# A fused layer of gated recurrence and mixture of experts: the order of the work ahead of the tile loop is rearranged

## The chip, the cores and the metric

The kernel runs on one core of a Trainium2 chip. It is written in Bass: every engine (TensorE = PE, VectorE = DVE, ScalarE = ACT, GpSimd = POOL, SyncE = SP for transfers) has its own list of instructions, executed in the order in which the code writes them, and the engines meet only at semaphores. The metric is the device time of one execution in microseconds; a smaller one is better. All data is float32.

## The reference

The input is 2 x 1024 tokens of width 256. They are normalised; the normalised rows `xn` feed a gated recurrence in log space and a mixture of 8 experts, two of which each token picks. The sum of input, recurrence and experts is the output.

```python
xn = _layernorm(x)
# attention replacement, over the whole sequence
k = xn @ W_z.T + b_z
log_z, log_coeffs = -softplus(-k), -softplus(k)
log_tilde_h = g_log(xn @ W_h.T + b_h)        # x >= 0: log(x + 0.5), else -softplus(-x)
a_star = pad(cumsum(log_coeffs, axis=-1))     # along the 256 channels
log_h = a_star + cumlogsumexp(concat(log_h0, log_z + log_tilde_h) - a_star, axis=1)
log_h = (log_h - log_h.mean()) / std(log_h, ddof=1)
attn = layernorm(exp(log_h)[:, 1:] + xn) * ln_w + ln_b
# experts
w, chosen = top_k(softmax(xn @ w_gate.T), 2); w = w / w.sum()
ffn = sum over e of (silu(xn @ w1[e].T) * (xn @ w3[e].T)) @ w2[e].T * weight of e for the token
out = x + attn + ffn
```

Each expert has 704 hidden columns.

## The kernel before

**The experts** run as a loop over tiles of 128 rows. 4096 (token, expert) pairs are sorted by expert with matmuls by one-hot matrices, and every expert gets whole tiles. Which tile belongs to which expert is data of the run, so the tile's expert is read from a table into registers. Tile `j` is gathered from DRAM (`gather`, POOL), transposed (`x_tile`, PE), split into a high and a low part (`x_hi` ACT, `x_lo` DVE), multiplied with the expert's first weights in three products (`up`, PE), gated (`silu` ACT, `gate` DVE), transposed (`h_tile`, PE), split (`h_hi` ACT, `h_lo` DVE), multiplied with the second weights (`down`, PE), copied and scattered. The weights too are split in high and low parts: an expert's weights are loaded into `raw` in 4 pieces and split into `wbuf` (high part: a copy, low part: a subtraction). `wbuf` holds two experts. When a later expert's pieces are split stands in a table `plan`, worked out on the chip by `tile_experts` and `tile_plan`: entry `j+1` says how many pieces are done after tile `j`. `AT = (0, 0, 1, 2)` are the tiles, counted from the start of the expert before, at which the four pieces are due; for the first expert the code adds one tile.

**Ahead of the loop** stands everything that this case is about:

1. Rows of `x` are loaded in 8 groups of 256 rows (`s_x`), the even ones in SP's queue, the odd ones in ACT's. DVE takes mean and variance (`bn_stats`), ACT the root, POOL and ACT the normalised rows.
2. PE transposes the rows in 8 pairs of tiles (index `m`), ACT copies them out of PSUM (`evacuate`), and PE makes the router's logits of the pair before (`logits`). Ahead of that PE runs `WARM` matmuls on a matrix of ones, whose result nobody reads.
3. DVE waits for all logits (`s_lg`) and works out the two experts of every token, PE ranks them (`rank_ps`), DVE makes the one-hot matrices, PE multiplies them (`table_ps`, 32 matmuls, in 8 lots of 4), DVE makes the tables of rows to gather and scatter (`gidx`, `sidx`, semaphore `s_idx`).
4. Meanwhile PE makes the projections of the recurrence: `project(c, mat)` for 4 chunks `c` of 512 tokens and `mat` 0 (k) and 1 (h), each 4 matmuls of 512 columns. ACT reads them (`k_part` two, `h_part` four instructions) and takes logarithms and exponentials (`k_log`, `h_log`, `h_exp`, `h_log1p`, on 1024 columns each). PSUM holds one k and one h projection, so PE waits until ACT has read the one before. Then `cumsum` on PE, and `softplus`, `add_cumsum`, `less_l2` and others on DVE.
5. The first tile: `up(0)`, `silu(0)`, `gate(0)`, `h_tile(0)`; the loop begins with `up(1)`. The rest of the recurrence's work is hung into the loop (functions `between` and `after`).

In SP's queue the loads of the first expert stand behind the rows of `x`:

```python
for q in range(PIECES - 1):
    sp.dma_start(raw[:, q * WP:(q + 1) * WP], w_main[0][:, q * WP:(q + 1) * WP]).then_inc(s_raw, 16)
```

The first expert's high parts are made by DVE, its low parts by POOL: two ahead of the gathers, two between them (`first_lo`).

## Time and profile before

| | before |
|---|---|
| median of 3 runs | 391.0 us (390.02 to 393.56) |
| the profiled execution: time, span | 389.11 us, 387.4 us |
| mean granted TensorE clock | 0.913 |
| busy: PE, DVE, ACT, POOL | 337.1, 267.2, 216.7, 212.5 us |
| start of `up(1)`, the loop's first matmul | 84.35 us |
| start of the last PE group, `down` of the last tile | 361.86 us |

The profiled execution is 1.9 us under the median; 1.7 us of its time lie outside of the span. Of the span 84 us are the stretch ahead of the loop, 277 us the loop, the remaining 25 us bring the experts' rows back and store the result. All times below are from the start of the span. Granted clock 1.00 is 2.4 GHz, 0.50 is 1.2 GHz.

### The profile page before, as it was taken

To read this page: it belongs to the slowest core of one execution; us is meant where nothing else is said; L and a number is where in the kernel's file an instruction comes from. 1 tells how busy PE (TensorE), PEld (TensorE's weight loads), DVE (VectorE), ACT (ScalarE), POOL (GpSimd) and SP (SyncE) were. 2 spreads that over 40 slices of the span, in tenths; PEclk is the share of its full clock that TensorE was granted. 3 is DMA by queue.
4 is the path that set the end of the run, shared out by engine and by line. 5 is a ranking of instruction groups with operands and counts; after the bars stand their busy time and mean duration, and the time that the engine had idled before them with its cause. 6 is when DMAs were issued, how large, how long until landed. Compare 5 with 4: busy or idle time off the path is not lost.

```text
span 387.4 us, 6792 instructions
## 1 busy us (share of the span) xinstructions
PE 337.1 (87%) x1896; PEld 283.4 (73%) x1896; DVE 267.2 (69%) x475; ACT 216.7 (56%) x327; POOL 212.5 (55%) x216
## 2 busy tenths in 40 slices
PE   6999999869879999989998979999999969999300
PEld 5895454449768888869897879999999958789300
DVE  4656889965946776995689944364649977863075
ACT  2431994755478995679894328975563644323100
POOL 6640027402874876897788768763875458441200
PEclk9556989989989999989999989999999989999955
DMA  7960004100432433133214366431432010111199
GB/s 267 399 218 0 0 3 124 52 15 14 118 100 91 123 108 93 42 118 98 86 41 139 97 206 199 154 106 43 143 96 97 28 30 29 42 43 30 53 310 317
DMA packets 22011, 41.37 MB, mean 107 GB/s; under 512 B 2481, under 2 KB 15281, under 8 KB 21969
## 3 DMA queue, kind: packets, MB, share of 16 engines
q1 hardware_dynamic: 14784, 26.74, 21.9%
q0 software_dynamic: 3728, 10.10, 8.4%
q10 hardware_dynamic: 3456, 3.94, 3.1%
q8 instruction: 29, 0.48, 0.5%
q14 instruction: 14, 0.11, 0.1%
HBM read 31.60 MB, written 9.18 MB: 105 GB/s over the span
## 4 chain that ended last, share of the span: by engine, by line
PE 68%; DVE 12%; DMA 7%; ACT 4%; issue 4%; POOL 3%; ACTq 1%; POOLq 1%; DVEq 0%
PE PS L1302 29%; PE PS L1317 15%; PE PS L1202 8%; PE PS L1329 6%; DMA xn<-x 3%; PE PS L1231 2%; DMA y_dram<-hst,scol 2%; PE PS L1269 2%; DVE xn L1177 2%; POOL wbuf L424 2%; DVE xn L1062 1%; DVE A L996 1%; DVE xn L1058 1%; DMA y_dram<-work,scol 1%; ACT hT L592 1%
## 5 line engine op out<-in xcount | busy, mean ns | idle before, releaser
L1302 PE MATMUL PS<-wbuf,xT 128*128 128x512 f32 (+1 forms) x648 | 152.7, 391 | 6.6 <-issue 3.9
L1302 PEld LDWEIGHTS PS<-wbuf,xT 128*128 128x128 f32 x648 | 121.1, 194 | 30.4 <-issue 9.4
L1317 PE MATMUL PS<-wbuf,hT 128*128 128x256 f32 x648 | 88.0, 290 | 2.5 <-DVE hT L957 2.3
L1317 PEld LDWEIGHTS PS<-wbuf,hT 128*128 128x128 f32 x648 | 80.3, 191 | 4.8 <-issue 4.7
L424 POOL TENSOR_TENSOR wbuf<-raw,wbuf x28 | 75.9, 2721 | 12.6 <-ACT wbuf L606 8.8
L957 DVE TENSOR_TENSOR hT<-PS,hT 128x768 fp32r<-128x768 f32 x36 | 34.4, 957 | 55.7 <-ACT hT L592 53.9
L405 POOL DMA_INDIRECT work<-xn_dram,gcol x39 | 50.2, 1288 | 30.2 <-POOL gcol L403 27.9
L597 ACT ACTIVATE tmp<-PS 128x512 f32<-128x512 f32 x72 | 32.1, 460 | 41.4 <-PE PS L1302 40.9
L962 DVE TENSOR_TENSOR tmp<-tmp,PS 128x512 f32<-128x512 f32 x72 | 34.8, 515 | 28.5 <-ACT tmp L597 27.4
L413 POOL DMA_INDIRECT y_dram<-work,scol x35 | 37.6, 1076 | 27.5 <-POOL scol L411 27.5
L1329 PE MATMUL PS<-ident,tmp 128*128 128x128 f32 x216 | 30.9, 281 | 10.9 <-DVE tmp L962 10.8
L592 ACT ACTIVATE hT<-PS 128x768 fp32r<-128x768 f32 x35 | 28.3, 810 | 17.3 <-PE PS L1329 17.3
L621 ACT ACTIVATE work<-PS 128x256 f32<-128x256 f32 x35 | 13.2, 378 | 44.0 <-PE PS L1317 42.6
L403 POOL COPY gcol<-gidx 128x1 uint32 (+1 forms) x39 | 17.3, 445 | 36.0 <-DVE sidx L896 30.6
L1329 PEld LDWEIGHTS PS<-ident,tmp 128*128 128x128 f32 x216 | 25.1, 144 | 12.5 <-DVE tmp L962 9.7
L1202 PE MATMUL PS<-xnT_M,small_sb 128*128 128x512 f32 x64 | 33.5, 677 | 0.0
L606 ACT ACTIVATE wbuf<-raw x28 | 30.4, 1109 | 3.8 <-issue 3.3
L411 POOL COPY scol<-sidx 128x1 uint32 (+1 forms) x35 | 9.2, 263 | 36.7 <-ACT work L621 36.6
L1202 PEld LDWEIGHTS PS<-xnT_M,small_sb 128*128 128x128 f32 x64 | 13.4, 218 | 16.0 <-issue 15.2
L705 ACT ACT_TABLE_LOAD x14 | 18.0, 1283 | 0.3
L713 ACT ACT_TABLE_LOAD x14 | 18.0, 1283 | 0.2
L578 ACT ACTIVATE xT<-PS 128x256 fp32r<-128x256 f32 x37 | 14.2, 382 | 5.0 <-PE PS L1269 5.0
(196 smaller groups left out, 420.9 us busy)
## 6 DMA issues: line engine op xcount, KB each, us to landing
raw<-w_main SPq DMA_DIRECT2D x24, 544.0 KB, 4.0
raw<-w_main SPq DMA_DIRECT2D x8, 416.0 KB, 3.3
xn_dram<-xn SPq DMA_DIRECT2D x4, 512.0 KB, 8.0
U<-x ACTq DMA_DIRECT2D x2, 1024.0 KB, 5.6
U<-y_dram SPq DMA_DIRECT2D x4, 512.0 KB, 5.4
A<-y_dram SPq DMA_DIRECT2D x4, 512.0 KB, 5.4
out<-xn SPq DMA_DIRECT2D x4, 512.0 KB, 3.6
xn<-x SPq DMA_DIRECT2D x4, 256.0 KB, 4.3
```

What stands on the lines that cost most here:

```text
L405: pool.indirect_dma_start(xg[:, k, :], None, xn_dram, bass.IndirectOffsetOnAxis(gcol[:, k:k + 1], 0)).then_inc(s_gt[k], 16)
L413: pool.indirect_dma_start(y_dram, bass.IndirectOffsetOnAxis(scol[:, k:k + 1], 0), ysb[:, k, :], None).then_inc(s_st[k], 16)
L424: pool.tensor_tensor(lo, raw[:, ds(part, WP)], hi.bitcast(fp32), ALU.subtract).then_inc(s_w, 1)
L592: act.activation(hT[:, 0, :], hT_ps, ACT.Copy).then_inc(s_hhi, 1)
L597: act.activation(sls[n], w1_ps[n], ACT.Silu).then_inc(s_silu, 1)
L606: act.activation(wslot(p // PIECES + 1, 0, part), raw[:, ds(part, WP)], ACT.Copy).then_inc(s_hi, 1)
L957: dve.tensor_tensor(hT[:, 1, :], hT_ps, hT[:, 0, :].bitcast(fp32), ALU.subtract).then_inc(s_hlo, 1)
L962: dve.tensor_tensor(g_hs[n], sls[n], w3_ps[n], ALU.mult).then_inc(s_g, 1)
L1202: ins = pe.matmul(PS[:, base + qo * CH:base + (qo + 1) * CH], wzh_sb[:, q, mat, qo * P:(qo + 1) * P], xnT[:, q, c * CH:(c + 1) * CH], star ...
L1302: ins = pe.matmul(PS[:, at:at + cols], xT[:, slot, xpart, q * P:(q + 1) * P], wbuf[:, w, wpart, q * 2 * F + at:q * 2 * F + at + cols], sta ...
L1317: ins = pe.matmul(y_ps, hT[:, hpart, c * P:(c + 1) * P], wbuf[:, w, wpart, W13 + c * D:W13 + (c + 1) * D], start=(c == 0 and hpart == 0 an ...
L1329: ins = pe.transpose(hT_ps[:, c * P:(c + 1) * P], g_h[:, a:a + P], ident[:, :])
```

## The change

Nothing is computed otherwise; instructions change their place, their engine or their number.

- PE: `WARM` goes from 56 to 96, and 8 more of these matmuls (`FILL`) follow the first two pairs of transposes. From the third pair on, one quarter of a projection (one matmul of 512 columns) stands between the transposes and the logits: six quarters, `project(0, 0)` and half of `project(0, 1)`. The other projections move up accordingly; `x_tile(1)` stands ahead of `cumsum(1)`. PE's wait for the plan becomes a wait for the experts' table.
- Loads: the small inputs go behind two groups of rows in ACT's queue, and SP's loads of the first expert wait until the projections' weights (`s_large`) have landed.
- First expert: the low parts are made by DVE right behind its high parts. POOL has only gathers left there.
- ACT: reads of projections go ahead of the logarithms; `x_hi(0)` and `x_hi(1)` go behind `k_log(3)`, and only `h_part(3)` is behind them.
- DVE: `x_lo`, `softplus(2)`, `add_cumsum(1)` and `gate(0)` go ahead of `tile_plan`; `tile_plan` goes behind `gate(0)`, and the weights of the two experts per token (`w12`) and `u0` behind `softplus(3)`. The scratch `due` moves from `hT` to the second half of `wbuf`.
- The second expert's pieces are due one tile earlier (`at` in place of `at + 1`).

```diff
-WARM = 56
+WARM = 96
+FILL = 8
-        due = hT[:, :, :].rearrange("p a n -> p (a n)")[:, 0:NCOL * 3 * (E - 1)]
+        due = wflat[:, 2 * WALL:2 * WALL + NCOL * 3 * (E - 1)]
@@ SP
+            sp.wait_ge(s_large, 16)
             for q in range(PIECES - 1):
@@ POOL
-            first_lo(0)
-            first_lo(1)
...
-            gather(0, 0)
-            first_lo(2)
-            gather(1, 1)
-            first_lo(3)
-            gather(2, 2)
-            gather(3, 3)
+            for j in range(DEEP):
+                gather(j, j)
@@ ACT
-            act.dma_start(small_sb[:, 0:FIRST], small[:, 0:FIRST]).then_inc(s_small, 16)
             for g in range(1, 8, 2):
+                if g == 5:
+                    act.dma_start(small_sb[:, 0:FIRST], small[:, 0:FIRST]).then_inc(s_small, 16)
@@ DVE
+            for q in range(PIECES):
+                dve.wait_ge(s_hi, q + 1)
+                hi, lo = (wbuf[:, 0, n, q * WP:(q + 1) * WP] for n in range(2))
+                dve.tensor_tensor(lo, raw[:, q * WP:(q + 1) * WP], hi.bitcast(fp32), ALU.subtract).then_inc(s_w, 1)
...
+                dve.sem_inc(s_eid, 1)
...
-                    ins = dve.tensor_scalar(when3[:, k, 0:1], tstart[:, 0:1], float(at + 1), None, ALU.add)
+                    ins = dve.tensor_scalar(when3[:, k, 0:1], tstart[:, 0:1], float(at), None, ALU.add)
@@ PE
                 ins.then_inc(s_xtr, 1)
+                if m < 2:
+                    warm(FILL)
+                else:
+                    if m == 2:
+                        pe.wait_ge(s_large, 16)
+                        pe.wait_ge(s_xnT, 2)
+                    project(0, (m - 2) // 4, ((m - 2) % 4,))
                 if m:
                     logits(m - 1)
...
-            pe.wait_ge(s_ctl, 1)
+            pe.wait_ge(s_eid, 1)
```

**PE, the last three pairs of transposes and what follows up to the ranks.** Line 1243 (1248 after) is a transpose, 1231 (1236) the logits, 1202 (1206) a projection, 1252 and 1253 (1264 and 1265) the ranks. Before:

```order
11 L1231 MATMUL PS<-small_sb,xnT_M 128x8 x4
12 L1243 MATMUL PS<-ident,xn 128x128 x4
13 L1231 MATMUL PS<-small_sb,xnT_M 128x8 x4
14 L1243 MATMUL PS<-ident,xn 128x128 x4
15 L1231 MATMUL PS<-small_sb,xnT_M 128x8 x8
16 L1202 MATMUL PS<-xnT_M,small_sb 128x512 x4
17 L1252 MATMUL PS<-pick_b,tri_b 128x128
18 L1253 MATMUL PS<-pick_b,ones_b 128x128
19 L1202 MATMUL PS<-xnT_M,small_sb 128x512 x12
```

After:

```order
18 L1236 MATMUL PS<-small_sb,xnT_M 128x8 x4
19 L1248 MATMUL PS<-ident,xn 128x128 x4
20 L1206 MATMUL PS<-xnT_M,small_sb 128x512
21 L1236 MATMUL PS<-small_sb,xnT_M 128x8 x4
22 L1248 MATMUL PS<-ident,xn 128x128 x4
23 L1206 MATMUL PS<-xnT_M,small_sb 128x512
24 L1236 MATMUL PS<-small_sb,xnT_M 128x8 x8
25 L1206 MATMUL PS<-xnT_M,small_sb 128x512 x6
26 L1264 MATMUL PS<-pick_b,tri_b 128x128
27 L1265 MATMUL PS<-pick_b,ones_b 128x128
28 L1206 MATMUL PS<-xnT_M,small_sb 128x512 x12
```

A matmul of 512 columns stands in every pair now, and six instead of four stand ahead of the ranks.

**PE, from the one-hot products (line 1261, 1273 after) to the first tile's `up` (1302, 1312 after).** 1212 to 1214 (1217 to 1219) are a cumulative sum, 1269 (1281) the transposes of a gathered tile. Before:

```order
20 L1261 MATMUL PS<-hT,xT 128x44 x32
21 L1202 MATMUL PS<-xnT_M,small_sb 128x512 x4
22 L1212 MATMUL PS<-A,tri 128x512
23 L1213 MATMUL PS<-A,ones 128x512
24 L1214 MATMUL PS<-A,tri 128x512
25 L1202 MATMUL PS<-xnT_M,small_sb 128x512 x4
26 L1269 MATMUL PS<-ident,work 128x128 x2
27 L1202 MATMUL PS<-xnT_M,small_sb 128x512 x4
...
31 L1269 MATMUL PS<-ident,work 128x128 x2
32 L1202 MATMUL PS<-xnT_M,small_sb 128x512 x4
33 L1302 MATMUL PS<-wbuf,xT 128x512 x12
```

After:

```order
29 L1273 MATMUL PS<-hT,xT 128x44 x32
30 L1206 MATMUL PS<-xnT_M,small_sb 128x512 x4
31 L1217 MATMUL PS<-A,tri 128x512
32 L1218 MATMUL PS<-A,ones 128x512
33 L1219 MATMUL PS<-A,tri 128x512
34 L1206 MATMUL PS<-xnT_M,small_sb 128x512 x4
35 L1281 MATMUL PS<-ident,work 128x128 x4
36 L1217 MATMUL PS<-A,tri 128x512
37 L1218 MATMUL PS<-A,ones 128x512
38 L1219 MATMUL PS<-A,tri 128x512
39 L1312 MATMUL PS<-wbuf,xT 128x512 x12
```

Of the four projections behind the one-hot products two are left.

**DVE, from the first tile's split to its second one.** Line 954 is `x_lo`, 963 `gate`, 871 to 878 `tile_plan`, 958 `h_lo`, 1082 to 1096 `w12` and `u0`. After:

```order
103 L954 TENSOR_TENSOR xT<-PS,xT 128x256
104 L963 TENSOR_TENSOR tmp<-tmp,PS 128x512
105 L963 TENSOR_TENSOR tmp<-tmp,PS 128x192
106 L871 TENSOR_TENSOR wbuf<-hst,iota_c 128x924
107 L874 TENSOR_REDUCE hst<-wbuf 128x44
...
111 L958 TENSOR_TENSOR hT<-PS,hT 128x768
112 L923 TENSOR_TENSOR U<-U,xnT_M 128x2x512
113 L917 SCALAR_TENSOR_TENSOR A<-U,A 128x2x512
114 L1082 TENSOR_SCALAR w<-w 128x16
...
121 L963 TENSOR_TENSOR tmp<-tmp,PS 128x512
```

Before, `tile_plan`, `w12` and `u0` stood ahead of the first `x_lo`; now the plan stands behind `gate(0)`, and `w12` and `u0` between `softplus(3)` and `gate(1)`.

## Rows read from the trace of the kernel before

**Rows 1.** The page, chain of work that ended last, shares by engine.

```profile
PE 68%; DVE 12%; DMA 7%; ACT 4%; issue 4%; POOL 3%; ACTq 1%; POOLq 1%; DVEq 0%
```

**Rows 2.** Windows of 1 us: busy (count) of PE, PEld, DVE, ACT, POOL; clock; DMA share; GB/s.

```profile
5.00:6.00 1.00, 1.00 (x15) 1.00 (x14) 0.23 (x1) 0.51 (x1) 1.00 (x3) 1.00 1.09 374
...
29.00:30.00 1.00, 1.00 (x7) 1.00 (x6) 0.00 (x0) 0.26 (x1) 0.00 (x0) 0.50 0.00 0
...
36.00:37.00 1.00, 1.00 (x5) 0.26 (x3) 0.00 (x0) 0.00 (x0) 0.00 (x0) 0.85 0.00 0
...
85.00:86.00 1.00, 1.00 (x4) 0.81 (x3) 1.00 (x2) 0.00 (x0) 0.00 (x0) 0.50 0.00 0
```

**Rows 3.** Timeline of PE up to the first projection: start, length, line, [idle before, releaser].

```profile
1.70 5.13 PE L1189 MATMUL PS<-ones_b 128*128 128x128 bf16 x56 [1.70 <-POOL tri_b L363]
8.91 1.99 PE L1243 MATMUL PS<-ident,xn 128*128 128x128 f32 x8 [2.07 <-POOL xn L389]
...
24.66 1.72 PE L1231 MATMUL PS<-small_sb,xnT_M 128*128 128x8 f32 x8
26.23 1.09 PE L1243 MATMUL PS<-ident,xn 128*128 128x128 f32 x4
...
30.39 6.61 PE L1202 MATMUL PS<-xnT_M,small_sb 128*128 128x512 f32 x8
```

**Rows 4.** Timeline of DVE up to the tables.

```profile
17.44 7.32 DVE L778 CAST wbuf<-raw 128x1088 fp32r<-128x1088 f32 x4 [1.26 <-DMA raw<-w_tail]
30.57 0.29 DVE L788 COPY work<-PS 128x128 f32<-128x128 f32 x1 [5.82 <-PE PS L1231]
...
37.15 0.29 DVE L814 COPY work<-PS 128x128 f32<-128x128 f32 x1 [1.39 <-PE PS L1253]
...
54.76 2.36 DVE L916 SCALAR_TENSOR_TENSOR A<-U,A 128x1024 f32<-128x1024 f32 x2
```

**Rows 5.** DMA of 0 to 20 us, one issue; tile `raw`, one group (ns min/median/max).

```profile
small_sb<-small ACTq DMA_DIRECT2D x1, 768.0 KB, 13.8
...
L778 DVE CAST wbuf<-raw x4: 707/1917/3008, 17.4 to 21.8; 128x1088 fp32r<-128x1088 f32 x4
```

**Rows 6.** Timeline of PE from the one-hot products to tile 4.

```profile
47.13 1.37 PE L1261 MATMUL PS<-hT,xT 128*128 128x44 f32 x8
...
52.72 5.38 PE L1202 MATMUL PS<-xnT_M,small_sb 128*128 128x512 f32 x8
...
70.50 3.60 PE L1202 MATMUL PS<-xnT_M,small_sb 128*128 128x512 f32 x8
75.80 4.08 PE L1302 MATMUL PS<-wbuf,xT 128*128 128x512 f32 x18 [1.71 <-issue]
...
84.35 5.54 PE L1302 MATMUL PS<-wbuf,xT 128*128 128x512 f32 x18 [1.04 <-issue]
...
110.99 5.64 PE L1302 MATMUL PS<-wbuf,xT 128*128 128x512 f32 x18 [2.35 <-POOL wbuf L424]
```

**Rows 7.** Timeline of DVE behind the tables.

```profile
58.14 2.49 DVE L853 TENSOR_SCALAR hst<-hst 128x44 f32<-128x44 f32 x1
...
61.81 3.23 DVE L864 TENSOR_TENSOR hst<-hst 128x21 f32<-128x21 f32 x1
...
69.95 1.12 DVE L870 TENSOR_TENSOR hT<-hst,iota_c 128x924 fp32r<-128x924 f32 x1
...
75.28 0.42 DVE L953 TENSOR_TENSOR xT<-PS,xT 128x256 fp32r<-128x256 f32 x1
```

**Rows 8.** Timeline of POOL, the last two subtractions of the first expert.

```profile
58.09 2.49 POOL L395 TENSOR_TENSOR wbuf<-raw,wbuf 128x1088 fp32r<-128x1088 f32 x1
...
62.49 2.50 POOL L395 TENSOR_TENSOR wbuf<-raw,wbuf 128x1088 fp32r<-128x1088 f32 x1
```

**Rows 9.** Timeline of ACT ahead of the first `silu`.

```profile
78.63 1.06 ACT L523 ACTIVATE A<-A 128x1024 f32<-128x1024 f32 x1
79.71 1.28 ACT L587 ACT_TABLE_LOAD   x1
```

More of the change, by code:

```diff
@@ L1069, in _ @@
             less_l2(1)
+            x_lo(0, 0, xT0_ps)
+            softplus(2)
+            add_cumsum(1)
+            x_lo(1, 1, xT1_ps)
+            gate(0)
             tile_plan()
+            h_lo(0)
+            add_l3(0)
+            softplus(3)
             dve.wait_ge(s_zex, 1)
@@ L1088, in _ @@
                                        u0t[:, 0, :], ALU.add))
-            x_lo(0, 0, xT0_ps)
-            softplus(2)
-            add_cumsum(1)
-            x_lo(1, 1, xT1_ps)
-            gate(0)
-            h_lo(0)
-            add_l3(0)
-            softplus(3)
             def between(j):
@@ L1187, in _, with warm, project @@
             pe.wait_ge(s_const, 5)
-            for _ in range(WARM):
-                pe.matmul(warm_ps, ones_b[:, :], ones_b[:, :], start=True, stop=True)
+            def warm(times):
+                for _ in range(times):
+                    pe.matmul(warm_ps, ones_b[:, :], ones_b[:, :], start=True, stop=True)
+            warm(WARM)
             pe.wait_ge(s_const, 13)
             pe.wait_ge(s_small, 16)
-            def project(c, mat):
+            def project(c, mat, parts=(0, 1, 2, 3)):
                 base = 2 * CH * mat
@@ L1247, in _ @@
             logits(NT // 2 - 1).then_inc(s_lg, 1)
-            pe.wait_ge(s_large, 16)
-            project(0, 0)
+            project(0, 1, (2, 3))
+            project(1, 0)
             pe.wait_ge(s_pick, 1)
```

70 lines of the change are left out of this document (34 added, 36 removed).

## The prediction

> **What bounds the kernel now.** I read the chain of waits first: 68% of the span lies on PE and 12% on DVE [rows 1], so the reader is to look for places where PE waits or runs at half clock. The timelines of PE, DVE and ACT ahead of 84.35 us come next, since the change touches only that stretch and the first tiles. They show four things. (1) The pairs of transposes and logits run from 8.91 to 30.39 us [rows 3], 21.5 us, at granted clock 0.50 (1.2 GHz) throughout, though PE counts as busy all the time [rows 2]; DVE waits 5.8 us for them [rows 4]. (2) From DVE's first routing instruction at 30.57 to the tables at 54.76 [rows 4] one chain of small DVE steps and PE products runs. (3) From 52.72 to 74.1 us PE does four projections and two cumulative sums back to back [rows 6]. (4) Between the end of the projections and the loop's first matmul at 84.35 PE works 5 us and waits 5.3: 1.71 for `x_lo(0)`, which stands behind `tile_plan` and `w12` on DVE [rows 6, 7], 2.6 for `silu(0)` behind a `k_log` and a table load [rows 9], 1.04 for the registers. Then `up(1)` runs at half clock [rows 2, 6], and `up(4)`, the second expert's first tile, waits 2.35 us for POOL's subtraction and is slow again (5.64 against 4.08) [rows 6].
>
> **Part by part.** The sum follows one point after another on the new path; each is my estimate from rows.
>
> *More warm matmuls, FILL.* 56 took 5.13 us [rows 3], 15 per us at the end [rows 2]: 40 more take 2.7 (at most 3.7), to 9.5 us (10.5). The first transposes begin 0.6 us later than at 8.91. This costs nothing: the third pair's projection waits for ACT's second `evacuate`, by ACT's order not before 12.8 us.
>
> *Loads.* `x`, constants and projections are 3.1 MB; at 374 GB/s [rows 2] that is 8.3 us, and they have landed at about 11 us; before, the last of them took 13.8 us from its issue, sharing with the expert's 2.2 MB [rows 5]. The last rows of `x` come earlier too, so DVE's statistics are no longer held up. The expert then needs 5.9 us and some 2 for issue and start: 18.8 us (17.4 as before [rows 4] to 21).
>
> *First expert's split on DVE.* The four copies took 7.32 us [rows 4], between 0.71 and 3.0 each [rows 5]; the slow ones ran beside POOL's subtractions. Alone: 4 x 0.71 = 2.8. The subtractions: two operands on 1024 columns take 1.18 [rows 4], on 1088 1.25, four 5.0. DVE is free at 18.8 + 7.8 = 26.6 us (25 to 29).
>
> *Quarters of projections between logits.* The crux is the clock. At full clock a projection takes 3.44 us (8 records in 3.60 [rows 6]), a quarter 0.86; at half 6.61 / 4 = 1.65 [rows 3]. A pair is 0.94 + 1.51 = 2.45 us at half clock [rows 3], at full half of that, 1.23. If the clock stays at 2.4 GHz, six pairs with quarters take 6 x 2.09 from 12.8 us, and the last logits end at 12.8 + 12.5 - 0.5 (the first one's transposes are done) + 0.75 = 25.6 us. If it is at 1.2 GHz, at 12.8 + 6 x 4.1 - 0.9 + 1.5 = 38 us. Before, 30.39. I take the full clock: what was there at half clock are transposes and products of 8 columns, and now the engine streams 512-column operands through about 40% of each pair and has no 2.07 us gap ahead of the first transposes, the gap after which the clock fell.
>
> The Trainium skill (TensorE: Matmul & The Clock Gate, "What's actually happening") says that the clock depends on how busy the engine has been lately. By busy time alone the clock should have come back between 17 and 30 us; the trace has 0.50 there with PE at 1.00 [rows 2], so the measurement decides that full occupancy with such small products is not enough, and the forecast isn't safe.
>
> *From the logits to the tables.* DVE starts at 26.6, the later of the two, against 30.57: **-4.0 us**. Its steps are as before; the wait for the rank (1.39 [rows 4]) goes, as PE ends its six quarters (5.2 us) just by then. Then three projections (10.3 us) stand ahead of the one-hot products as before, now the later of the two inputs: products at 26.6 + 5.4 + 10.4 = 42.4 against 47.13 [rows 6]. The tables are ready at 50.0 against 54.7: **-0.7** beyond the 4.0.
>
> *Behind the tables.* PE has two projections instead of four, because 1.5 were made among the logits and half of one is made ahead of the ranks or between: 2 x 3.44 = **-6.9**. `up(0)` then starts at 62.4 us. Does ACT keep up? From its third k and h reads (43.1 us) it has 6 reads (3.7) and 12 wide instructions at 1.04 (each like 78.63 [rows 9], overlapping a little), so `x_hi(0)` at 59.3, and PE has the tile transposed at 59.5. Slack is nil; a late ACT costs its lateness. DVE: `tile_experts` had two instructions of 2.49 and 3.23 us that need 0.2, each beside a POOL subtraction of 2.5 that starts with it [rows 7, 8]; without these DVE saves 5.3 and has `x_lo(0)` at 61.2, before `up(0)`. The wait of **-1.7** goes. `silu(0)` has no `k_log` in front, the table is loaded (1.28 us [rows 9]) at 64.0, `up(0)`'s end is at 66.3, `silu`, `gate` and `h_tile` are done 1.3 us later instead of 3.4: **-2.1**. `up(1)` starts at 68.9 against 84.35. Sum: 4.0 + 0.7 + 6.9 + 1.7 + 2.1 = 15.4.
>
> *Plan behind the first gate.* `tile_plan` is 3.3 us on DVE (from 69.95 [rows 7]). Queued behind it are `h_lo(0)` and ACT's `h_hi(0)` and `silu(1)`, whose waits come first. `h_lo(0)` is done 5 us after `gate(0)`, PE needs it for `down(0)` after `h_tile` (0.7), the registers (1.04) and `up(1)` (3.9 or more): hidden by 0.6 us. Behind it stand two recurrence steps and `w12`, `u0` (2.0 us), and only then `gate(1)`. ACT has two pieces to split (2.1) ahead of `silu(1)`. So `h_tile(1)` waits 2 us where it waited none: tile 1 takes 9.3 us against 8.3 (84.35 to 92.7), of which a full clock in `up(1)` has given 1.5 back. **+1.0**, and up to +4 if POOL's two subtractions (2.5 each) block DVE's `softplus(3)` and `w12` as in [rows 7, 8].
>
> Beside this the Trainium skill (SBUF — State Buffer, "SBUF: two separate sides") says that DVE and GpSimd share a port pair that one of them holds for a whole instruction. The trace agrees (2.49 us for 44 columns). By that rule all of DVE's two-operand steps in tile 1 would wait for both subtractions, the upper bound of +4, and not half of it.
>
> *Pieces one tile earlier.* `up(4)` no longer waits 2.35 us and, without the gap, runs at full clock, 1.5 us faster: **-3.9**, of which I take 2.5, since the third and fourth piece collide with DVE in tiles 2 and 3 as they did before. Everything else in the loop is tied to tile numbers and moves along; PE is the bound there.
>
> Together 15.4 - 1.0 + 2.5 = 16.9 off 389.1: 372.2 us in the profiled execution; the median of the runs is 1.9 above it: **374 us**.
>
> **The rivals.**
> *A collision in tiles 0 to 2, or a late ACT.* The clock holds, but tile 1 takes 12 us, or `x_hi(0)` is late by 2 to 4: 3 to 7 us of the gain go: 377 to 382. For it: two collisions in [rows 7, 8]; against: POOL's other subtractions are gone.
> *The clock stays at 1.2 GHz among the logits.* They end at 38 us; of the next six quarters four are slow (6.6 + 1.7), so the ranks come at 46.4, the products at 56.8, the tables at 64.4 (before 54.7), and with the same 18.9 us behind them `up(1)` at 83.3. 1 us gained there and 1.5 to 3 in the first tiles: 385 to 388. For it: clock 0.50 from 9 to 36 us before; against: what is between the products now.
> *Slower.* The clock stays down not only there but until the one-hot products are over, since PE waits briefly for ACT's reads (one k and one h projection in PSUM) between projections. Then 18 quarters instead of four run at 1.65: 14 x 0.79 = 11 us more, `up(1)` at 94, and with 3 us back in the first tiles 396 us. It decides from 3 us of lost time on (rival two's 385 to 388 against 391). Against it: before, 6 us of projections brought the clock back (at 36 us [rows 2]) with the same reads behind them.
>
> **How the numbers follow.** Forecast (371 to 377) 0.60; collision or late ACT 0.17; clock low among the logits 0.18; slower 0.05. The likeliest gives 374. The range takes the first three cases: 369 (all of the 3.9 in `up(4)`, early loads) to 388. 1% (3.9 us) is about what a measurement can tell: faster than 387.1 are the first two and a third or half of the next, 0.84; within 1% the rest of it, 0.11; slower 0.05.
>
> **What would show it.** The granted clock between 12 and 26 us at 1.00; DVE's first routing step near 26.6 (if it comes at 38, the clock failed; if DVE is busy until then, the loads); its copies at 0.7 us; no idle PE ahead of the first `up`; `up(1)` near 69 and at full clock; no wait at the second expert's first tile. The prediction is wrong if the clock falls, or if ACT's queue, not PE, ends last ahead of `up(0)`.

## The result, and the profile after

The changed kernel takes 379.3 us (median of 4 runs, 378.1 to 381.0) against 392.1 us (4 runs, 390.0 to 393.6; the 391.0 above are the first three of them): ratio 0.968, 95% interval 0.961 to 0.975, **12.8 us faster**, by the interval 10 to 15. Here and below, single executions more than 1.5% above the fastest of their kernel are left out of medians and ratios (one each of e_load and e_fill0, and two of the kernel before in later rounds). The profiled execution took 378.11 us with a span of 376.2 and a mean granted clock of 0.943.

The starts of `up(j)` on PE's timeline split the gain by place:

| | before | after | difference |
|---|---|---|---|
| `up(0)` starts | 75.8 | 63.4 | -12.4 |
| tile 0, `up(0)` to `up(1)` | 8.5 | 7.1 | -1.4 |
| tile 1 | 8.3 | 13.6 | +5.3 |
| tile 2 | 8.8 | 8.8 | -0.1 |
| tiles 3 and 4 | 19.6 | 15.4 | -4.2 |
| `up(5)` to the end of the span | 266.3 | 267.9 | +1.6 |
| span | 387.4 | 376.2 | -11.2 |

So everything was gained ahead of the loop's first matmul `up(1)` (13.8 us), and the loop and what follows it lost 2.6; the first five tiles together gave 0.4 us.

The chain of waits of the changed kernel by engine, answering [rows 1]. PE's share is 7 points smaller and DVE's 8 larger. The chain now runs over the projections' weights (landed at 12.34 us), SP's wait for them, the first expert's load (21.46) and DVE's split and routing up to 33.86, then over PE up to `up(0)`, and over DVE again in tile 1. The logits are not on it.

```profile
PE 61%; DVE 20%; DMA 7%; ACT 6%; issue 4%; ACTq 1%; SPq 1%; DVEq 0%; POOL 0%; POOLq 0%
```

Windows of 1 us, columns as in [rows 2]: clock 1.00 among the logits (16 to 17 us), no transfers at all at 12 to 13, and clock 0.50 right behind the one-hot products, at 50 us.

```profile
12.00:13.00 1.00, 0.53 (x2) 0.30 (x2) 0.60 (x6) 0.72 (x2) 1.00 (x2) 1.00 0.00 0
16.00:17.00 1.00, 1.00 (x11) 1.00 (x11) 0.00 (x0) 0.00 (x0) 0.00 (x0) 1.00 1.00 392
50.00:51.00 1.00, 1.00 (x2) 0.34 (x1) 0.85 (x5) 1.00 (x3) 0.00 (x0) 0.50 0.00 0
```

PE's timeline up to the ranks, answering [rows 3]. The first quarter starts at 12.57, the logits end near 25.9 (30.4 before), and then PE waits 2.60 us for the picked experts.

```profile
1.71 7.27 PE L1192 MATMUL PS<-ones_b 128*128 128x128 bf16 x96 [1.71 <-POOL tri_b L366]
...
12.57 1.10 PE L1206 MATMUL PS<-xnT_M,small_sb 128*128 128x512 f32 x2 [0.47 <-ACT xnT_M L502]
...
24.21 1.85 PE L1236 MATMUL PS<-small_sb,xnT_M 128*128 128x8 f32 x16
25.91 5.40 PE L1206 MATMUL PS<-xnT_M,small_sb 128*128 128x512 f32 x12
33.91 0.23 PE L1264 MATMUL PS<-pick_b,tri_b 128*128 128x128 bf16 x1 [2.60 <-DVE pick_b L808]
```

DVE's timeline up to the first routing step, answering [rows 4]: it waits 8.15 us for the first expert, splits it in 7.4 us and starts routing at 28.84.

```profile
21.49 2.63 DVE L774 CAST wbuf<-raw 128x1088 fp32r<-128x1088 f32 x4 [8.15 <-DMA raw<-w_tail]
24.04 4.89 DVE L778 TENSOR_TENSOR wbuf<-raw,wbuf 128x1088 fp32r<-128x1088 f32 x4
28.84 0.28 DVE L788 COPY work<-PS 128x128 f32<-128x128 f32 x1
```

The load of the projections' weights, answering [rows 5]: 8.9 us from issue to landing (13.8 before).

```profile
small_sb<-small ACTq DMA_DIRECT2D x1, 768.0 KB, 8.9
```

PE's timeline from the one-hot products on, answering [rows 6]. `up(0)` waits for nothing, `up(1)` runs at full clock (4.12 us), and the transposes of tile 1's hidden rows wait 5.92 us for `gate(1)`; behind that gap `up(2)` runs at half clock (5.53).

```profile
44.18 1.23 PE L1273 MATMUL PS<-hT,xT 128*128 128x44 f32 x8
...
63.41 4.42 PE L1312 MATMUL PS<-wbuf,xT 128*128 128x512 f32 x18
...
70.52 4.12 PE L1312 MATMUL PS<-wbuf,xT 128*128 128x512 f32 x18 [1.31 <-issue]
...
82.91 1.54 PE L1339 MATMUL PS<-ident,tmp 128*128 128x128 f32 x6 [5.92 <-DVE tmp L963]
84.11 5.53 PE L1312 MATMUL PS<-wbuf,xT 128*128 128x512 f32 x18
```

DVE's timeline from the first `x_lo` on, answering [rows 7]. The two steps of `tile_experts` that took 2.49 and 3.23 us are short now (0.19, 0.18); in exchange two steps of `w12` on 16 columns take 2.48 and 2.11.

```profile
54.99 0.19 DVE L853 TENSOR_SCALAR hst<-hst 128x44 f32<-128x44 f32 x1
...
62.49 0.42 DVE L954 TENSOR_TENSOR xT<-PS,xT 128x256 fp32r<-128x256 f32 x1
...
75.82 2.48 DVE L1082 TENSOR_SCALAR w<-w 128x16 f32<-128x16 f32 x1
...
78.62 2.11 DVE L1084 TENSOR_TENSOR w<-w 128x16 f32<-128x16 f32 x1
...
82.17 0.95 DVE L963 TENSOR_TENSOR tmp<-tmp,PS 128x512 f32<-128x512 f32 x2
```

POOL's timeline beside them, answering [rows 8]: the first two pieces of the second expert. Their two subtractions cover just those two steps.

```profile
75.44 5.26 POOL L421 TENSOR_TENSOR wbuf<-raw,wbuf  x2 [12.01 <-ACT wbuf L602]
```

ACT's timeline, answering [rows 9]: `x_hi` follows PE's transposes at once, no `k_log` behind it, and a table load ends ahead of `silu(0)`.

```profile
61.22 0.66 ACT L570 ACTIVATE xT<-PS 128x256 fp32r<-128x256 f32 x2 [0.54 <-PE PS L1281]
...
64.21 1.28 ACT L583 ACT_TABLE_LOAD   x1
```

### The profile page after: what moved, and what is told of

It is laid out like the page before. It is cut to its first block, busy times and chain, and to the rows that moved or that the text cites. A ratio compares the mean times of both kernels' runs of the same rounds, so it can differ in the third digit from the quotient of the medians.

```text
span 376.2 us, 6906 instructions
## 1 busy us (share of the span) xinstructions
PE 326.8 (87%) x1952; PEld 277.1 (74%) x1952; DVE 265.1 (70%) x479; ACT 216.4 (58%) x327; POOL 198.8 (53%) x212
## 4 chain that ended last, share of the span: by engine, by line
PE 61%; DVE 20%; DMA 7%; ACT 6%; issue 4%; ACTq 1%; SPq 1%; DVEq 0%; POOL 0%; POOLq 0%
PE PS L1312 28%; PE PS L1327 16%; PE PS L1339 6%; PE PS L1206 5%; DMA small_sb<-small 2%; DVE xn L1059 2%; DMA y_dram<-hst,scol 2%; DMA raw<-w_tail 2%; DVE xn L1178 2%; ACT hT L588 2%; PE PS L1281 2%; DVE tmp L963 1%; DVE A L997 1%; DVE wbuf L778 1%; DVE hT L958 1%
## 5 line engine op out<-in xcount | busy, mean ns | idle before, releaser
L1312 PEld LDWEIGHTS PS<-wbuf,xT 128*128 128x128 f32 x648 | 119.9, 192 | 25.8 <-issue 5.2
L1327 PE MATMUL PS<-wbuf,hT 128*128 128x256 f32 x648 | 89.9, 294 | 2.5 <-DVE hT L958 2.4
L1327 PEld LDWEIGHTS PS<-wbuf,hT 128*128 128x128 f32 x648 | 82.2, 195 | 4.8 <-issue 4.8
L402 POOL DMA_INDIRECT work<-xn_dram,gcol x39 | 42.7, 1095 | 29.9 <-POOL gcol L400 22.2
L410 POOL DMA_INDIRECT y_dram<-work,scol x35 | 38.5, 1100 | 27.5 <-POOL scol L408 25.2
L400 POOL COPY gcol<-gidx 128x1 uint32 (+1 forms) x39 | 20.5, 526 | 39.3 <-DVE sidx L897 36.8
L602 ACT ACTIVATE wbuf<-raw x28 | 30.4, 1110 | 4.3 <-issue 3.9
L1206 PE MATMUL PS<-xnT_M,small_sb 128*128 128x512 f32 x64 | 31.1, 626 | 0.5 <-ACT xnT_M L502 0.5
L408 POOL COPY scol<-sidx 128x1 uint32 (+1 forms) x35 | 10.3, 295 | 25.0 <-ACT work L617 25.0
L1206 PEld LDWEIGHTS PS<-xnT_M,small_sb 128*128 128x128 f32 x64 | 12.1, 200 | 12.8 <-issue 12.1
L1059 DVE TENSOR_TENSOR xn<-xn,small_sb 128x512 f32<-128x512 f32 x16 | 15.5, 970 | 0.5
```

Source lines behind the costliest of these rows:

```text
L402: pool.indirect_dma_start(xg[:, k, :], None, xn_dram, bass.IndirectOffsetOnAxis(gcol[:, k:k + 1], 0)).then_inc(s_gt[k], 16)
L410: pool.indirect_dma_start(y_dram, bass.IndirectOffsetOnAxis(scol[:, k:k + 1], 0), ysb[:, k, :], None).then_inc(s_st[k], 16)
L602: act.activation(wslot(p // PIECES + 1, 0, part), raw[:, ds(part, WP)], ACT.Copy).then_inc(s_hi, 1)
L1206: ins = pe.matmul(PS[:, base + qo * CH:base + (qo + 1) * CH], wzh_sb[:, q, mat, qo * P:(qo + 1) * P], xnT[:, q, c * CH:(c + 1) * CH], star ...
L1312: ins = pe.matmul(PS[:, at:at + cols], xT[:, slot, xpart, q * P:(q + 1) * P], wbuf[:, w, wpart, q * 2 * F + at:q * 2 * F + at + cols], sta ...
L1327: ins = pe.matmul(y_ps, hT[:, hpart, c * P:(c + 1) * P], wbuf[:, w, wpart, W13 + c * D:W13 + (c + 1) * D], start=(c == 0 and hpart == 0 an ...
```

## The experiments

Each is the changed kernel with the edit shown. Ratios are against the kernel before, measured on the same chip; the changed kernel itself was measured only once, with 4 runs, so two kernels are told apart by their ratios, and two ratios whose intervals overlap are not. "Tiles 0-4" is from `up(0)` to `up(5)`, "rest" from there to the end of the span, both of the profiled execution (of e_load its longest, 388.25 us).

| | median us (range) | ratio (95%) | `up(0)` | tiles 0-4 | rest |
|---|---|---|---|---|---|
| before | 392.1 (390.0-393.6) | 1 | 75.8 | 45.3 | 266.3 |
| changed | 379.3 (378.1-381.0) | 0.968 (0.961-0.975) | 63.4 | 44.9 | 267.9 |
| e_noq | 393.7 (392.7-398.2) | 1.009 (1.004-1.013) | 78.9 | 46.2 | 265.6 |
| e_noq_warm56 | 393.7 (392.0-396.7) | 1.009 (1.005-1.012) | 78.9 | 46.0 | 265.7 |
| e_warm56 | 386.3 (384.6-387.6) | 0.986 (0.982-0.991) | 66.8 | 45.0 | 273.9 |
| e_fill0 | 379.9 (379.3-382.6) | 0.975 (0.969-0.980) | 65.5 | 44.9 | 267.0 |
| e_load | 378.9 (376.8-382.4) | 0.974 (0.964-0.983) | 72.8 | 44.9 | 268.5 |
| e_poollo | 386.2 (383.6-388.7) | 0.989 (0.980-0.999) | 71.5 | 45.6 | 269.2 |
| e_plan | 378.2 (376.4-378.5) | 0.969 (0.962-0.976) | 68.5 | 38.9 | 269.3 |
| e_w12 | 382.3 (381.0-383.9) | 0.977 (0.972-0.982) | 65.4 | 39.1 | 276.9 |
| e_at1 | 379.3 (379.1-379.7) | 0.969 (0.966-0.973) | 67.3 | 44.3 | 266.0 |
| e_w12at1 | 377.0 (373.5-378.4) | 0.965 (0.956-0.974) | 63.0 | 43.8 | 269.0 |
| e_fillrank | 383.7 (380.6-384.9) | 0.981 (0.975-0.986) | 64.1 | 44.9 | 272.9 |
| e_best | 378.9 (375.9-380.7) | 0.969 (0.964-0.974) | 66.7 | 44.0 | 267.4 |

**e_noq: the projections back to their old places.** Warm-up, fill and all else as changed. That includes ACT's new order and the place of the first tile's transposes behind the last projection; before the change they stood behind `project(2, 1)`, with two projections more to come.

```diff
-                else:
-                    ...
-                    project(0, (m - 2) // 4, ((m - 2) % 4,))
...
-            project(0, 1, (2, 3))
-            project(1, 0)
+            project(0, 0)
             pe.wait_ge(s_pick, 1)
...
+            project(0, 1)
+            project(1, 0)
             project(1, 1)
-            project(2, 0)
-            project(2, 1)
...
+            project(2, 0)
+            cumsum(0)
+            project(2, 1)
             project(3, 0)
-            cumsum(0)
             project(3, 1)
             x_tile(0, 0, 16, xT0_ps)
```

> The changed kernel with PE's projections in the places of before: none among the logits, one ahead of the ranks, three ahead of the one-hot products, four behind. Warm matmuls and all else as changed. Theory A (the quarters keep the clock up among the logits): granted clock falls to 0.50 between 9 and 16 us and stays there until the projections, the last logits end near 29 to 30 us instead of 25.9. Rival B (the absence of a gap ahead of the first transposes keeps the clock up, not the quarters): clock 1.00 among the logits, which then end near 21 us, bounded by ACT and POOL; DVE still starts at 28.8, since it splits the first expert. In both the four projections behind the tables cost 6.9 us there: up(1) 6 to 9 us later than the changed kernel's 70.5 under B, 7 to 11 under A.

The whole gain is gone, and more than either theory said: `up(1)` came at 87.1, 16.6 us later than in the changed kernel. Nor did the logits end at 29 to 30 or near 21 us, as they had it. The windows of e_noq show why this isn't only the clock: with the long warm-up it stays at 1.00 until about 17 us and then drops.

```profile
12.00:16.00 4.00, 3.73 (x34) 3.46 (x33) 1.14 (x10) 2.52 (x6) 2.91 (x6) 1.00 0.61 210
16.00:20.00 4.00, 4.00 (x28) 4.00 (x27) 0.00 (x0) 1.45 (x3) 0.00 (x0) 0.67 0.98 323
20.00:24.00 4.00, 4.00 (x21) 4.00 (x21) 2.84 (x5) 2.12 (x3) 0.00 (x0) 0.50 1.08 384
```

PE was 100% busy in the last two rows with transposes and products of 8 columns only, and the clock fell under it; with quarters between them it stays at 1.00 (the row at 16 us of the changed kernel). That is what the quarters do to the clock. Yet the logits of e_noq end at 25.2 us, no later than with the quarters. What is lost is the projections' work. One and a half of them stood among the logits at no cost; without that PE has four projections behind the one-hot products and transposes the first tile at 68.8 us (60.8). Then PE waits 6.91 us more for `x_lo(0)`, and that wait is ACT's: in its new order `h_part(2)` stands ahead of the logarithms of chunks 0 and 1, so ACT is idle for 5.84 and 4.74 us until the late projections come, and only behind all logarithms up to `k_log(3)` does it read the first tile (`x_hi(0)`, line 570). Its rows, and DVE's `x_lo(0)`:

```profile
62.11 1.27 ACT L523 ACTIVATE xnT_M<-PS,small_sb 128x512 f32<-128x512 f32 x2 [4.74 <-PE PS L1206]
...
77.93 0.64 ACT L570 ACTIVATE xT<-PS 128x256 fp32r<-128x256 f32 x2
```

```profile
78.33 0.42 DVE L954 TENSOR_TENSOR xT<-PS,xT 128x256 fp32r<-128x256 f32 x1 [6.58 <-ACT xT L570]
```

So the two projections are paid for twice, and the second time because ACT's new order counts on having them early; in the kernel before, ACT read the first tile at 64.36. No run has the projections in their old places with ACT's old order, so what the interleaving is worth by itself is not shown.

**e_noq_warm56: all of PE's edits ahead of the ranks undone.** As e_noq, and `WARM = 56`, `FILL = 0`.

> The changed kernel with all of PE's edits ahead of the ranks undone: the projections where they stood before (none among the logits), 56 warm matmuls and none behind the pairs. Left of the change are the loads, the split of the first expert on DVE, ACT's order, the plan behind the first gate and the pieces. Theory A (without the quarters the rest is worth nothing or less, since the clock is low among the logits and DVE starts the routing as late as before): the clock is 0.50 from 9 to 33 us, the logits end at 30 to 31.5, the routing starts at 30.5 to 31.5, up(0) at 79 to 82, and 393 to 397 us, slower than before by 0.5 to 1.5%. Theory B (the rest keeps its own gains, the 1.7 us of waiting ahead of up(0), 2.1 at the first silu and 2.5 at the second expert's pieces): up(0) at 74 to 76 and 385 to 388 us.

The same 393.7 us as e_noq, as the first theory says. The clock was 0.50 from about 13 us to 30 and the logits ended at 27.7 (30 to 31.5 forecast) instead of 25.2, but that mattered to nobody: DVE was splitting the first expert until 28.91. PE then waits 6.92 us for `x_lo(0)` as in e_noq.

```profile
78.92 5.37 PE L1309 MATMUL PS<-wbuf,xT 128*128 128x512 f32 x18 [6.92 <-DVE xT L954]
```

So without the interleaving, the other edits together (loads, split on DVE, ACT's order, plan, pieces) make the kernel 0.9% slower. Which of them does is not shown apart; the 6.92 us above stand behind ACT's order.

**e_warm56: the quarters, but the short warm-up.** `WARM = 56`, `FILL = 0`.

> The changed kernel with 56 warm matmuls and no FILL; quarters stay. Theory A (the quarters alone hold or bring back the clock): the clock falls at most for a few us after the warm matmuls and is 1.00 from about 16 us on; the time is within 1 us of the changed kernel. Rival B (without the longer warm-up the clock falls ahead of the first quarter, and pairs with a quarter are too light to bring it back): 0.50 from 9 to 30 us, logits end at 36 to 38 us, the time is 5 to 10 us above the changed kernel.

The clock fell near 13 us and came back near 19.5 with the quarters running:

```profile
16.00:20.00 4.00, 4.00 (x16) 2.97 (x17) 0.00 (x0) 0.60 (x1) 0.00 (x0) 0.54 1.00 356
20.00:24.00 4.00, 4.00 (x28) 3.04 (x27) 2.70 (x5) 1.19 (x2) 0.00 (x0) 1.00 1.09 386
```

The time is the rival's, but its mechanism is not: pairs with a quarter did bring the clock back. The logits ended at 29.5 and `up(0)` started 3.4 us later than in the changed kernel. Of the other 6 us (273.9 against 267.9), 3.5 were lost in tiles 15 to 19, see e_fillrank, and 2.0 behind the start of the last tile's `up`. e_fill0, next, differs from this kernel only by its 40 more warm matmuls: there the clock held.

**e_fill0: long warm-up, no fill.** `FILL = 0`.

> The changed kernel without the 8 matmuls of ones behind each of the first two pairs of transposes (WARM stays at 96). Theory A (the long warm-up alone bridges the start, the quarters do the rest): the gap ahead of the first quarter grows from 0.47 us to 1.4 to 1.7, the clock stays 1.00 until 49 us, up(0) at 63 to 64, and 379 us. Theory B (any idle time over 1 us ahead of the first quarter lets the clock fall, as the 2.04 us did in the run in which the weights were late, and the half clock then holds for 3 to 16 us): clock 0.50 from 12 or 13 us on, the logits end at 28 to 35, up(0) at 66 to 72, and 383 to 388 us.

The clock held among the logits, as the first theory says, but not for its gap of 1.4 to 1.7 us: PE was idle for 0.25 us ahead of the first logits and 0.43 ahead of the first quarter, against 0.47 in all in the changed kernel. `up(0)` was 2 us later because the wait ahead of the ranks was 2.83 us in this execution and the clock fell in it. 379.9 us against 379.3: the fill is worth nothing that can be told.

```profile
12.81 1.10 PE L1206 MATMUL PS<-xnT_M,small_sb 128*128 128x512 f32 x2 [0.43 <-ACT xnT_M L502]
...
34.38 0.29 PE L1264 MATMUL PS<-pick_b,tri_b 128*128 128x128 bf16 x1 [2.83 <-DVE pick_b L808]
```

**e_load: SP doesn't wait for the projections' weights.**

```diff
-            sp.wait_ge(s_large, 16)
+            sp.wait_ge(s_x[6], 16)
```

> The changed kernel, but SP's loads of the first expert wait for the last rows of x (the group that ends SP's share) and no longer for the projections' weights. In the changed kernel the copies on DVE waited until 21.49 us for the load and were followed by the routing at 28.84; PE then waited 2.60 us for the picked experts ahead of the ranks, and in two other kernels the clock fell in that gap. Theory A (the late load is worth its lateness): raw lands at 17.5 to 18.5, the copies and subtractions end by 25.9, the routing starts right behind the logits at 25.9, PE waits under 0.5 us ahead of the ranks; up(0) at 60 to 61 (63.4 before), the same start of every later tile less 2.5 to 3, and 376 to 377 us. Theory B (the copies share DVE with the statistics of the last rows, and the projections' weights share the transfer with the expert's 2.2 MB): the weights land later than 12.4, the first quarter starts 1 to 3 us later than 12.57, the logits end at 27 to 29, up(0) at 63 to 65, and 379 to 381 us. Theory C (the prologue gains but the loop's collisions between POOL's and DVE's subtractions fall otherwise): up(0) at 60 to 61 and 378 to 380 us.

The times decide nothing: the median is 378.9, and the executions from 376.8 to 382.4 us spread over the times of all three theories. The only trace is of the longest one, 388.25 us. In it the expert landed 1.8 us earlier (copies at 19.69), but the projections' weights some 1.5 us later (13.95), as the second theory says, and it shows what such a lateness can do. PE waited 2.04 us for the weights, the clock fell in the window from 15 to 16 us and stayed down for 17 us in spite of the quarters; the logits ended at 35.6. PE's row at the first quarter, and two windows:

```profile
13.95 1.12 PE L1206 MATMUL PS<-xnT_M,small_sb 128*128 128x512 f32 x2 [2.04 <-DMA small_sb<-small]
```

```profile
20.00:24.00 4.00, 4.00 (x15) 2.97 (x15) 4.00 (x6) 0.60 (x1) 0.00 (x0) 0.50 0.70 249
...
28.00:32.00 4.00, 4.00 (x14) 2.97 (x15) 0.00 (x0) 0.60 (x1) 0.00 (x0) 0.50 0.81 320
```

This execution is the prediction's rival of the low clock, which forecast the logits at 38 us and 385 to 388. So SP's wait, during which transfers stand still at 12 to 13 us, may guard the weights and with them the clock. What it is worth on the whole is not shown: the kernel without it has about the same median.

**e_poollo: POOL makes the first expert's low parts, as before.**

```diff
+            first_lo(0)
+            first_lo(1)
             pool.wait_ge(s_idx, 1)
...
-            for q in range(PIECES):
-                dve.wait_ge(s_hi, q + 1)
-                ...
```

> The changed kernel, but POOL makes the low parts of the first expert, two ahead of the gathers and two between them, as before the change. Theory A (the split on DVE costs nothing that another place would not cost more): DVE has 4.9 us less ahead of the routing, but its copies run beside POOL's subtractions (0.7 to 3 us each); the routing starts at 25.9 to 27 in place of 28.84. Behind the tables the two instructions of tile_experts that took 0.19 and 0.18 us take 2.5 to 3.2 again, x_lo(0) comes 5 us later than it could, and up(0) starts at 64 to 67 with a wait for it: 380 to 384 us. Theory B (only the place of DVE's work ahead of the routing counts): up(0) at 60.5 to 61.5 us, and 376 to 378 us.

386.2 us, more than the first theory's 380 to 384, with `up(0)` at 71.5 instead of its 64 to 67. DVE saved no time ahead of the routing: its four copies took 7.23 us beside POOL's subtractions, and the routing started at 29.65 (28.84). The two collisions in `tile_experts` came back, and `up(0)` was 8 us later. DVE's rows, and POOL's beside them (`first_lo` is L398 here, `tile_experts` L859 and L871):

```profile
57.49 2.50 DVE L859 TENSOR_SCALAR hst<-hst 128x44 f32<-128x44 f32 x1
...
61.38 3.02 DVE L871 TENSOR_TENSOR hst<-hst 128x21 f32<-128x21 f32 x1
```

```profile
57.44 2.50 POOL L398 TENSOR_TENSOR wbuf<-raw,wbuf 128x1088 fp32r<-128x1088 f32 x1
...
61.85 2.49 POOL L398 TENSOR_TENSOR wbuf<-raw,wbuf 128x1088 fp32r<-128x1088 f32 x1
```

**e_plan: DVE's order of before behind the tables**, `tile_plan`, `w12` and `u0` ahead of `x_lo(0)`.

> The changed kernel with DVE's order of before behind the tables: tile_plan, w12 and u0 ahead of x_lo(0), softplus(2), add_cumsum(1) and gate(0) behind them. Theory A (the plan behind the first gate moved work from ahead of up(0) into tile 1): x_lo(0) is 5.5 us later than at 62.49, up(0) starts at 68.0 to 69.5 in place of 63.4, tile 1 then takes 7.3 to 8.3 us in place of 13.6, since nothing but h_lo(0), two recurrence steps and gate(1) is left there; up(2) at 83 to 85 (84.1 in the changed kernel), and 378 to 381 us: the change of place is worth nothing in the end. Theory B (what stands ahead of up(0) costs its full time, and tile 1 collides with POOL's subtractions anyhow): up(0) at 68 to 69, tile 1 at 11 us or more, up(2) at 88 or later, and 382 to 385 us.

The first theory: `up(0)` waits and starts 5.0 us later, tile 1 takes 6.9 us instead of 13.6, `up(2)` starts at 84.68 (84.11), and the time is the same (378.2 us). Moving the plan behind the first gate moved 5 us of DVE's work from ahead of `up(0)` into tile 1 and gained nothing.

```profile
68.45 6.68 PE L1313 MATMUL PS<-wbuf,xT 128*128 128x512 f32 x18 [4.36 <-issue]
...
77.81 4.11 PE L1313 MATMUL PS<-wbuf,xT 128*128 128x512 f32 x18 [1.44 <-issue]
...
84.68 4.09 PE L1313 MATMUL PS<-wbuf,xT 128*128 128x512 f32 x18
```

**e_w12: `w12` behind tile 20, `u0` behind `tile_experts`**, so that neither stands in tile 1.

```diff
             def between(j):
+                if j == 20:
+                    pair_weights()
```

> The changed kernel, with w12 and u0 taken from between softplus(3) and gate(1): u0 behind tile_experts, w12 into tile 20. Theory A (in tile 1 PE waits 5.9 us because w12's small DVE steps are caught behind POOL's two subtractions, ahead of gate(1)): the wait at h_tile(1) goes but for what softplus(3) and the two subtractions still cost, tile 1 (up(1) to up(2)) falls from 13.6 to 7.5 to 8.5 us, up(2) keeps the full clock, and the kernel gains 5 to 7 us on the changed one: 371 to 374 where the changed one has 378 to 381. Rival B (tile 1 is held by ACT, which splits two pieces ahead of silu(1), or by the subtractions blocking softplus(3) just as well): tile 1 stays above 11 us, gain under 2 us.

Tile 1 took 7.2 us, tiles 0-4 5.8 less, so the collision and its price are as read. But the gain of 5 to 7 us did not come: 382.3 us, longer than the changed kernel by the ranges, though the intervals of the two ratios overlap. In the profiled execution `up(0)` was 2.0 us later (PE waited 2.74 us ahead of the ranks and the clock fell), and the rest took 276.9 us instead of 267.9. 5.6 of the 9 us lie in tiles 15 to 19, 4.4 in tiles 5 to 14, and the tiles behind won 1.1 back. DVE's large steps in tiles 15 to 17 now met POOL's subtractions head on, 4.73, 3.59 and 3.60 us for a step that took 1.22 alone, and PE waited for the gates behind them. DVE, POOL and PE of e_w12:

```profile
188.21 4.73 DVE L997 TENSOR_TENSOR A<-U,A 128x1024 f32<-128x1024 f32 x1
```

```profile
186.81 5.04 POOL L421 TENSOR_TENSOR wbuf<-raw,wbuf  x2
```

```profile
194.90 0.87 PE L1342 MATMUL PS<-ident,tmp 128*128 128x128 f32 x6 [2.02 <-DVE tmp L963]
```

**e_at1: the second and later experts' pieces one tile later**, as before the change (`float(at + 1)`).

> The changed kernel with the second expert's pieces due one tile later, as before. Theory A (the earlier pieces cause tile 1's collision and remove up(4)'s wait): tile 1 falls from 13.6 to about 8.5 to 9.5 us, and the collision moves to tile 2, where up(4) waits for POOL again 2 to 3 us and runs slow: up(5) starts 1 to 4 us earlier than the changed kernel's 108.3. Rival B (the earlier pieces are what the change earns in the loop): up(5) starts 2 us or more later than 108.3.

379.3 us, the same. As the first theory says, tile 1 took 9.3 us, since POOL's subtractions started only at 86.4, but `up(4)` waited 2.47 us for a piece again and ran at half clock. So the 4.2 us gained in tiles 3 and 4 and the 4.3 us lost in tile 1 have one cause in this order of DVE's work, the pieces' date. With the plan and `w12` out of tile 1 the early pieces cost nothing there (e_plan: tile 1 6.9 us, tiles 3 and 4 15.6). The other finding is in PE's row ahead of the ranks: after 3.28 us of idle time the clock had fallen, which it hadn't after the 2.60 us of the changed kernel, and `up(0)` came at 67.3; for that reason `up(5)` came 3.3 us later than in the changed kernel, which proves neither theory.

```profile
34.77 0.29 PE L1264 MATMUL PS<-pick_b,tri_b 128*128 128x128 bf16 x1 [3.28 <-DVE pick_b L808]
...
101.44 5.65 PE L1312 MATMUL PS<-wbuf,xT 128*128 128x512 f32 x18 [2.47 <-POOL wbuf L421]
```

**e_w12at1: both moves.**

> The changed kernel with both moves that each took the collision out of tile 1: w12 behind tile 20 and u0 behind tile_experts, and the second expert's pieces due one tile later. Alone the first gave 382.3 us (up(2) at 79.7, later collisions of POOL's subtraction with the recurrence steps in tiles 14 to 16) and the second 379.3 us. Theory A (the losses in tiles 7 to 20 come from where POOL's pieces fall against DVE's recurrence steps, which w12 behind tile 20 moves): up(1) at 72 to 74, tile 1 at 7.2 us, up(4) at 97 to 98 with a wait of 1 to 2.5 us for the pieces, losses in tiles 13 to 16 as in the first: 381 to 384 us. Theory B (the losses there are chance of the phase): up(5) at 105 to 107 and 374 to 378 us.

377.0 us, and the range (373.5 to 378.4) holds the shortest run of all kernels. Tile 1 took 8.4 us, tiles 3 and 4 19.7, as before the change, and the rest 269.0: the losses of e_w12 were not there, so they are no property of `w12`'s place alone (against the first theory), and the second theory's 105 to 107 for `up(5)` (106.8) and 374 to 378 us held.

**e_fillrank: 28 matmuls of ones ahead of the ranks**, where PE waits.

```diff
+            for _ in range(28):
+                pe.matmul(rank_ps, ones_b[:, :], ones_b[:, :], start=True, stop=True)
             pe.matmul(rank_ps, tri_b[:, :], pick_b[:, :], start=True, stop=True)
```

> The changed kernel with 28 more matmuls of ones (1.9 to 2.1 us at the rate of the warm ones, 96 in 7.27 us) between the projections and the ranks, where PE waits 2.2 to 3.3 us for the picked experts. Nobody reads their result. Theory A (the clock falls in that gap in some executions, as in the profiled ones of two experiments, and that costs 2 to 4 us there): the clock is 1.00 from the first quarter to 49 us in the profiled run, up(0) at 63.4 or less in it, and the median of the runs lies at 376.5 to 378.5 us with a spread under 3 us. Theory B (the fall in the gap is paid for by something else, such as ACT being late for x_hi(0) and x_hi(1) anyway): 379 to 380 us as the changed kernel, no matter what the clock does there.

Both theories failed. The wait shrank to 0.39 us and the clock held there, `up(0)` at 64.1, but the time was 383.7 us, 4 more than the changed kernel (ratios 0.981 and 0.968, whose intervals just touch). Tiles 0-4 are alike (44.9); the loss is in the rest (+5.0, 3.4 of it in tiles 15 to 19), as in e_warm56. A step of 1024 columns in tile 15 starts 1.15 us later than in the changed kernel, POOL's two subtractions at the same time (186.3), and it takes 4.55 instead of 3.07; the next two take 2.93 and 3.44 instead of 1.21 and 1.28. DVE and POOL of e_fillrank, then DVE of the changed kernel:

```profile
187.90 4.55 DVE L997 TENSOR_TENSOR A<-U,A 128x1024 f32<-128x1024 f32 x1
```

```profile
186.30 5.06 POOL L421 TENSOR_TENSOR wbuf<-raw,wbuf  x2
```

```profile
186.75 3.07 DVE L997 TENSOR_TENSOR A<-U,A 128x1024 f32<-128x1024 f32 x1
```

**e_best: e_w12at1 with these matmuls.**

> The changed kernel with w12 behind tile 20, u0 behind tile_experts, the second expert's pieces one tile later (376.96 us so far) and the 28 matmuls of ones ahead of the ranks. Theory A (each takes away a wait of its own): clock 1.00 up to 49 us, up(0) at 63.0, up(2) at 78.4, up(5) at 106.8, and 374.5 to 377 us with a spread under 3 us. Theory B (the gap's clock was not what spread the runs of the kernel without them, 373.45 to 378.4): 376 to 378 us with the same spread of 4 to 5 us.

378.9 us, not better than e_w12at1 and with the same spread; the first expert landed 2 us later than there in the profiled execution (copies at 23.16), PE still waited 2.11 us ahead of the ranks, behind which the clock held, and `up(0)` came at 66.7, not 63.0. The first theory failed. That the clock in the gap doesn't spread the runs fits the second, but only one of the six executions has a trace, so it is not shown. No kernel tried is surely faster than the changed one: e_w12at1's interval (0.956 to 0.974) holds 0.968.

## Why the prediction held, and where its terms were off

The range (369 to 388) holds 379.3, but the likeliest case (371 to 377, given 0.60) does not; the time is that of the rival with the collision (377 to 382, given 0.17), and its mechanism is that rival's too. The range held because it was wide enough for three cases. For the profiled execution the sum was 372.2, and it took 378.1. By the prediction's steps:

- **The clock among the logits: right.** 1.00 throughout, last logits at about 25.9 (25.6 forecast). Without the quarters it fell (e_noq), and with them but the short warm-up it fell too (e_warm56), so it took both. In e_load, once fallen, it stayed down for 17 us, in e_warm56 for some 6, with the same pairs. **But it was not what bounded the start of the routing.** DVE waited for the expert, not for the logits, and in e_noq_warm56, at 0.50 and without the quarters, it starts at 28.91 just the same. A fall of the clock costs only with the quarters in (logits at 35.6 in e_load). The text called this the crux; what the interleaving brings is the projections' time.
- **DVE free at 26.6: 28.84, off by 2.2.** The split took what was forecast (7.4 against 7.8), but the expert landed at 21.5, not 18.8. So the term of -4.0 measured -1.7. SP's wait let the transfers stand still near 12 to 13 us, which I had allowed for with "some 2", and the weights it waits for landed at 12.3, not 11. DVE's wait for the rank did go (0.21 us, before 1.39); instead PE was idle for 2.60 us ahead of the ranks, and since its three projections stand behind them, 1.8 us of the lateness were still there at the one-hot products (44.18 against 42.4).
- **Two projections less behind the tables, -6.9: right.** From the first one-hot product to the end of PE's work ahead of `up(0)` it was 27.0 us before and is 19.8 now. In e_noq, which has the two there, the first tile is transposed 8.0 us later: the products start 0.3 earlier, the half clock behind them costs 1.4 more, and 6.9 are left. `up(0)` waited for nothing and started at 63.4, 1.0 later than forecast, so 0.8 of the 1.8 was made up behind the products. What the text didn't see is how much hangs on this step once ACT has its new order: without it `up(0)` is 15.5 us later (e_noq).
- **`x_lo(0)` no longer late, -1.7: right**, for the reason given (no collision in `tile_experts`; e_poollo brings them back). **`silu(0)`: -1.4 in tile 0, not -2.1**, the registers' wait being 1.31 against 1.04 and `up(0)` itself 4.42 us long against 4.08.
- **Tile 1, +1.0: the step that failed.** It measured +5.3. The price of the collision was in the text as "up to +4", and it came in full, on top of the +1.0: two subtractions, two blocked steps of 2.48 and 2.11 us that took 0.17 and 0.18 before, together 4.2. The Trainium skill (SBUF — State Buffer, "SBUF: two separate sides") makes it the rule that whichever of the two engines starts first keeps the shared pair for its whole instruction, where DVE's step has two inputs in SBUF or runs in a two-port mode. The trace agrees for the step with two inputs (line 1084, 2.11 us for 16 columns); the one of 2.48 us (line 1082) has one input, and whether it ran in such a mode no trace shows. The mistake was to add the plan, the pieces and `w12` each by itself: the pieces' earlier date is what put POOL's first work into the tile in which DVE had `w12` and `tile_plan` to make up (e_at1: 9.3 us, e_w12: 7.2, e_plan: 6.9).
- **Pieces one tile earlier, -2.5 of 3.9: they gave -4.2**, and cost 4.3 in tile 1. Net nothing (e_at1).
- **"Everything else in the loop moves along": off by +1.6** here (1.2 in tiles 30 to 34, 1.0 behind them, 0.6 won before), and by 5 to 9 us more in e_warm56, e_fillrank and e_w12. It was wrong above all for tiles 15 to 19, where large steps of POOL and DVE meet.
- **The rivals' times stand on two scales.** 377 to 382 is the median; 385 to 388 comes from 389.1 less 2.5 to 4.0, so it is 385.1 to 386.6 for the profiled execution and 387 to 388.5 for the median, and the 396 is the profiled execution's too. The range's upper end, 388, does not quite hold the second rival's median.

What stays open: why the clock came back after 6 us in one kernel and 17 in another with the same work, and what sets the phase between POOL's pieces and DVE's steps in tiles 15 to 19. Nor did any edit aim at the half clock behind the one-hot products: it lasted 3.4 us before, in the changed kernel, e_fill0 and e_w12, and 6.8 us in e_noq, e_at1, e_warm56, e_fillrank and e_best, and half of the 3.4 us more, 1.7, is my estimate of what that moved `up(0)`. That tiles 15 to 19 take 3.4 to 5.6 us more where DVE's steps are blocked is read from the traces; that a shift of about 1 us in the loop's start brings it about was not tried by itself.
